# Two-batch gated cross-attention block on one core: 68 turns of the identity taken out of TensorE's order

## What is computed

```python
x = x + tanh(g_xattn[0]) * L0_xattn(ctx, layernorm(x), ...)   # 77 + 512 keys, 8 heads of 64, queries = tokens
x = x + tanh(g_ffn[0])   * L0_ffn(layernorm(x), ...)          # quantised linear 128->512, conv of 3, silu, quantised 512->128
x = x + tanh(g_xattn[1]) * L1_xattn(layernorm(x), ctx, ctx)   # 77 keys, 16 heads of 8, rotary
x = x + tanh(g_ffn[1])   * L1_ffn(layernorm(x), ...)          # 8 experts of 64, top 2, and a shared one
```

## The kernel before, in words

| place | turns | ahead of | bank |
|---|---|---|---|
| 1 | 8 | the first `k` projection (L592, L594) | 2 |
| 2 | 18 | `f1` of batch 1, its four turns of XN; an `a1` with two more follows | 7 |
| 3 | 5 | an `a4` front (L681) | 6 |
| 4 | 11 | an `a4` back (turns of S) | 2 |
| 5 | 5 | an `a4` back | 4 |
| 6 | 4 | an `a4` front | 4 |
| 7 | 11 | an `a4` back | 3 |
| 8 | 6 | an `a4` back | 2 |

## Time and profile before

### The profile page before, as it was taken

How to read it: one execution, slowest core, us unless ns; L and a number is a source line. 1 busy time by engine, 2 the same in 40 slices (tenths; PEclk the granted TensorE clock), 3 DMA queues, 4 the chain that set the end, 5 groups by cost and what they waited for, 6 DMA issues and landing times.

```text
span 271.9 us, 5419 instructions
## 1 busy us (share of the span) xinstructions
PE 248.7 (91%) x1754; PEld 183.7 (68%) x1754; DVE 230.7 (85%) x561; ACT 184.0 (68%) x462; POOL 32.3 (12%) x57
## 2 busy tenths in 40 slices
PE   0999999999999999999999999968868899899996
PEld 0757687787688866677678878745545565657665
DVE  5699969886679976999989789899999999998781
ACT  2596668776577557868879862159799596773561
POOL 3100000000001010000000021320002302133230
PEclk9999999999999999999999999999999999999999
DMA  6198620030300003300300000000000000000001
GB/s 203 38 251 298 159 58 2 0 91 0 91 0 1 4 0 89 91 0 4 89 0 4 0 2 0 4 0 0 1 2 2 2 0 4 0 10 4 29 0 41
DMA packets 8848, 10.70 MB, mean 39 GB/s; under 512 B 1115, under 2 KB 5877, under 8 KB 8821
## 3 DMA queue, kind: packets, MB, share of 16 engines
q1 hardware_dynamic: 7792, 9.70, 13.4%
q10 hardware_dynamic: 1029, 0.65, 0.8%
HBM read 4.99 MB, written 0.52 MB: 20 GB/s over the span
## 4 chain that ended last, share of the span: by engine, by line
PE 62%; DVE 23%; issue 7%; ACT 6%; DMA 1%; DVEq 0%; ACTq 0%
PE slot L535 18%; PE slot L621 11%; PE slot L602 6%; PE slot L603 5%; PE slot L580 3%; PE slot L762 3%; PE slot L628 2%; PE slot L586 2%; DVE nm L1063 2%; ACT S L916 2%; DVE mx L1172 2%; ACT PR L842 2%; PE slot L756 2%; PE slot L592 1%; PE slot L713 1%
## 5 line engine op out<-in xcount | busy, mean ns | idle before, releaser
L842 ACT ACTIVATE PR<-slot,nm 128x589 f32<-128x589 f32 x64 | 47.5, 749 | 14.7 <-DVE nm L1063 12.5
L1063 DVE TENSOR_REDUCE nm<-slot 128x1 f32<-128x589 f32 x64 | 46.4, 763 | 3.7 <-PE slot L603 3.2
L535 PE MATMUL slot<-K,PR 128*128 128x128 f32 (+1 forms) x320 | 44.4, 278 | 1.6 <-ACT PR L842 1.5
L535 PEld LDWEIGHTS slot<-K,PR 128*128 128x128 f32 (+1 forms) x320 | 35.5, 142 | 12.3 <-ACT PR L842 9.6
L602 PE MATMUL slot<-KH,Q 128*128 128x296 f32 (+1 forms) x128 | 40.7, 336 | 0.8 <-DVE PT L779 0.4
L621 PE MATMUL slot<-PT,V 128*64 128x256 f32 (+1 forms) x320 | 38.1, 384 | 0.0
L603 PE MATMUL slot<-KL,Q 128*128 128x296 f32 (+1 forms) x128 | 36.2, 299 | 0.0
L621 PEld LDWEIGHTS slot<-PT,V 128*64 128x64 f32 (+1 forms) x320 | 21.6, 137 | 11.9 <-issue 2.7
L602 PEld LDWEIGHTS slot<-KH,Q 128*128 128x128 f32 x128 | 24.1, 189 | 5.5 <-issue 2.1
L777 ACT ACTIVATE PT<-slot 128x640 f32<-128x640 f32 x34 | 23.5, 704 | 6.5 <-PE slot L535 5.8
L779 DVE COPY PT<-slot 128x640 f32<-128x640 f32 x30 | 24.4, 820 | 2.7 <-PE slot L535 2.3
(11 more groups left out here) (170 smaller groups left out, 500.8 us busy)
## 6 DMA issues: line engine op xcount, KB each, us to landing
KH<-KH SPq DMA_DIRECT2D x16, 147.5 KB, 2.5
KL<-KL SPq DMA_DIRECT2D x16, 147.5 KB, 2.5
CTT<-in_ctxT SPq DMA_DIRECT2D x1, 640.0 KB, 7.8
K<-in_const SPq DMA_DIRECT2D x1, 589.0 KB, 8.8
WGU<-in_wgu SPq DMA_DIRECT2D x1, 580.0 KB, 8.6
out<-X SPq DMA_DIRECT2D x8, 64.0 KB, 1.5
L1W<-in_l1w SPq DMA_DIRECT2D x1, 384.0 KB, 3.6
WD<-in_wdT SPq DMA_DIRECT2D x1, 320.0 KB, 11.3
```

Of the source, the lines that this page charges most:

```text
L535: return pe.transpose(dst, src, ident[0:p, 0:p])
L842: act.activation(PR[:, s, :], W[:, K0:K0 + KEYS0], ACT.Exp, bias=nm0[:, s:s + 1], accum_out=sum0[:, b, p * 2 + f, t, e:e + 1]).then_inc(pr ...
L1063: dve.tensor_reduce(nm0[:, s:s + 1], W[:, K0:K0 + KEYS0], AX.X, ALU.max, negate=True).then_inc(max_ready, 1)
```

## The change

The eight additions are cut from the words of `PLAN`; its later lines are wrapped anew, which makes the diff long, and no word changes its place. Two lines of it as they stood and stand:

```diff
-x0:F0 x0:A1 k:F2+8@2 x0:D2 q:F4 k:A1 k:F0 q:A1 k:D1 v:F6 x0:P2 k:A1 q:D1 v:F2 v:Ca k:D1 q:F5 v:Ca u:F6 x0:D3
+x0:F0 x0:A1 k:F2 x0:D2 q:F4 k:A1 k:F0 q:A1 k:D1 v:F6 x0:P2 k:A1 q:D1 v:F2 v:Ca k:D1 q:F5 v:Ca u:F6 x0:D3
...
-a3:P1 f4:B f4:B o:D1 a4:F2 f4:D2 a4:F0 n:P2 f4:D2 a4:F4 n:D3 f4:P2 f4:D3 f1:F6+18@7 a4:D1 a1:F7 f1:A1 a4:D1
+a3:P1 f4:B f4:B o:D1 a4:F2 f4:D2 a4:F0 n:P2 f4:D2 a4:F4 n:D3 f4:P2 f4:D3 f1:F6 a4:D1 a1:F7 f1:A1 a4:D1 a1:A1
```

More of the change, by code:

```diff
@@ L127 @@
 u:B u:Ca a3:F2 n:P2 u:Cd n:D3 w:F4 a3:D1 a3:F0 w:A1 w:D1 a3:P1 f4:F5 a3:D1 f4:F6 f4:A1 o:F7 f4:A1 o:F4 o:D1
-a3:P1 f4:B f4:B o:D1 a4:F2 f4:D2 a4:F0 n:P2 f4:D2 a4:F4 n:D3 f4:P2 f4:D3 f1:F6+18@7 a4:D1 a1:F7 f1:A1 a4:D1
-a1:A1 a4:A1 a2:F7 a1:P1 f1:D1 a2:D1 f2:F6 a4:A1 a4:B a4:D1 f2:A1 f2:F7 a4:D3 a4:Ca a4:B f2:A1 f2:D1 f2:F2
-f2:F3 a4:Ca f2:A1 a4:F0 f2:D1 f2:A1 f2:A2 f2:D1 a4:F6+5@6 f2:A2 a4:A1 f2:D1 f2:D2 a4:B+11@2 f2:D2 f2:A2
-a4:D1 f2:A2 a4:Ca a4:F2 f2:D2 a4:A1 f2:D2 a4:B+5@4 a4:D1 f3:F4 a4:Ca a4:D1 f3:F5 a4:A1 a4:F0 f3:D1 f3:D1
@@ new lines @@
+a4:A1 a2:F7 a1:P1 f1:D1 a2:D1 f2:F6 a4:A1 a4:B a4:D1 f2:A1 f2:F7 a4:D3 a4:Ca a4:B f2:A1 f2:D1 f2:F2 f2:F3
+a4:Ca f2:A1 a4:F0 f2:D1 f2:A1 f2:A2 f2:D1 a4:F6 f2:A2 a4:A1 f2:D1 f2:D2 a4:B f2:D2 f2:A2 a4:D1 f2:A2 a4:Ca
+a4:F2 f2:D2 a4:A1 f2:D2 a4:B a4:D1 f3:F4 a4:Ca a4:D1 f3:F5 a4:A1 a4:F0 f3:D1 f3:D1 f3:A1 a4:B a4:A1 f3:Cd
+f3:F4 a4:D3 f3:A1 a4:B a4:D3 a4:Ca f4:F5 f3:Ca a6:D0 f3:F6 f3:D1 a6:P1 f4:A1 f4:F7 f4:A1 f4:B f3:D1 f3:A1
+f4:B a4:Ca a6:F4 f4:D2 f3:A1 f4:D2 f3:Ca f3:Ca a4:D1 f4:F6 f4:P2 a6:A1 a4:F2 f4:A1 a6:D1 f4:F5 f4:D3 a4:A1
@@ new lines @@
+f4:B a6:B a4:D1 a1:F7 a6:D2 a1:A1 a4:B f4:A1 a1:P1 a4:A1 a2:F7 f4:D2 a6:P2 a4:Ca f4:B a2:D1 a4:B a4:Ca a6:D3
+a4:F6 f4:D2 m1:F4 a4:F0 a4:D1 m1:A1 f4:P2 m3:F2 a4:D1 a4:A1 a4:F4 m3:D1 a4:A1 f4:D3 a4:B a4:D3 m3:A1 a4:B
+a4:Ca a4:D3 a1:F3 a4:Ca m2:F6 a4:D1 a1:A1 m3:D2 a1:P1 a4:F0 a4:A1 m2:B a2:F3 a4:D1 m2:A1 a4:B m2:A2 m2:P1
+a2:D1 a4:A1 a4:Ca a4:B a6:D0 a4:F4 a4:D3 a6:P1 a4:Ca a6:F2 m2:D1 a6:D0 a4:D1 a4:F0 m2:D2 a6:A1 a6:P1 a4:A1
+a6:D1 a4:F6 a4:D1 a6:B a6:F3 a4:D1 a4:A1 a6:D2 a4:A1 a4:B a4:B a4:Cd a6:P2 a4:Cd a4:F4 a6:A1 a6:D3 a4:B
@@ new lines @@
+a6:D1 m1:F2 a4:D3 a4:Ca m4:F0 a4:D1 a6:B m1:A1 m4:A1 m3:F2 m2:F6 a6:D2 a4:A1 m4:B m2:A1 m2:P1 a4:D3 a4:B
+m4:D2 m2:B a6:P2 a6:D0 a4:Ca m3:D1 a6:P1 m2:F0 m2:A2 a6:D3 m3:A1 m2:F4 m2:A1 m2:D1 m3:D2 m1:F3 m2:A1 m2:B
+m1:A1 m2:B m2:A2 m2:D2 a6:F3 m2:P1 m2:A2 m2:P1 m2:D1 m4:F6 a6:A1 m2:D2 m3:F2 a6:D1 m4:A1 m4:F0 m2:D1 a6:B
+m3:D1 m4:A1 m4:B a6:D2 m3:A1 m4:B m4:D2 a6:P2 m2:D2 m2:F6 m4:D2 a6:D3 m4:F0 m3:D2 m2:A1 m2:B m4:A1 m1:F3
+m2:A2 m4:B m1:A1 m2:P1 m3:F4 m4:D2 m2:F2 m2:D1 m3:D1 m2:F0 m2:A1 m2:D2 m2:P1 m2:B m3:A1 m2:A1 m3:D2 m2:F6
@@ L147 @@
+m2:A2 m2:B m2:A1 m2:D1 m2:P1 m4:F4 m2:A2 m2:B m2:D2 m4:A1 m2:P1 m2:D1 m4:F2 m2:A2 m2:D2 m4:B m4:A1 m2:D1
+m2:D2 m4:F0 m4:D2 m4:B m4:A1 m4:F6 m4:D2 m4:B m4:A1 m4:B m4:D2 m4:D2
 """
```

## The result

The changed kernel took 276.86 us (median of 20 runs, 275.90 to 278.28), the kernel before 275.71 us (20 runs, 273.50 to 278.29). The ratio is 1.0054, 95% interval 1.0028 to 1.0080: slower, by about 1.5 us, and far inside 2%. It leaves out the three runs of the kernel before at 278.1 to 278.3 us, more than 1.5% above its fastest; over all runs the means are 276.8 and 275.9 us, 0.9 us apart. The forecast of 276.6 us in 273.2 to 282.5 holds. What stands behind it holds in part only, and the experiments show that the kernel before is not as steady as its one profile makes it look.

The account below looks back on a forecast made before the run. The prediction took VectorE and ScalarE, not TensorE, to set the pace around most of the turns. Its terms, -0.3 + 1.2 + 0.8 = +1.7 us, on the median 274.93 gave 276.6 us, range 273.2 to 282.5.

Parts of the forecast that it names:

- The seven later places: Sixty turns between 175.93 and 225.16 us; the next instruction waits for data, so removing them gains 0 as work.
- place 2: 18 turns from 175.93 to 177.95 us; gain 0 as work, but removal leaves a 3.2 us hole until 179.41.
- place 6: Four turns, the next instruction at 213.49 us after 0.93 us idle; gain 0.
- place 4: Eleven turns at 189.94 us, the next instruction at 191.61 waiting for ScalarE; gain 0, but removal leaves a 2.3 us hole.
- The clock falls in the new holes and soon mends: Likeliest case: a fall or two between about 179 and 191 us, each soon mended; 276.6 us, chance 0.48.
- the clock holds: Rival: TensorE's clock stays whole through the new holes; 274.5 us, chance 0.30.
- stays low to 208 us: Rival: the clock falls and stays low through the sparse part, 179 to 208 us; costs 7, 281.6 us, chance 0.20.
- if low clock reaches beyond 208 us: Sign that was to show the rival of a long low stretch, forecast at 281.6 us, chance 0.20.
- place 1: Eight turns before the first K projection, 7.62 to 9.32 us; removal gains 0.3, up to 0.6, or loses 1.4 net.
- The price of a fall: Low clock from 179.4 us costs 1.2 (bounds 0 to 3.3), from about 191 us 0.8 (bounds 0 to 1.8).
- L673's room: L673 at 180.96 us takes 0.9 us more at low clock; VectorE takes it up only at 182.90, cost next to 0.
- I put the change on the median: Whole kernel: adds +1.7 us to the runs' median of 274.93, not the profiled 273.79, giving 276.6 us.

Follow-up runs that it names:

- a kernel with 80 turns: The kernel before with 12 turns more in its longest hole, ahead of 198.97 us, against the kernel before: ratio 0.9970 (0.9926 to 1.0013).
- the full cover: The kernel before with turns added in every hole that has a free bank, against the kernel before: ratios 0.9967 and 0.9992; median 274.44 us in one set.

## Why the prediction was right or wrong

- **The seven later places bring nothing back as work: right.** Every instruction behind them still waits for the same data: 180.40 for VectorE's L1304, 189.94 for YC, 193.16 and 200.92 for ScalarE's S, 215.24 for Q. TensorE's idle time ahead of them grew by about what the turns had taken (1.08 to 2.87 us at place 2, 0.93 to 1.36 at place 6; at place 4 from 0.61 and 0.25 around the turns to 2.43).
- **The clock falls in the new holes and soon mends: right.** It was forecast for most executions and came in all 26 (by their mean clocks). The rival "the clock holds" is out by that, and the rival "stays low to 208 us", forecast at 281.6, by three stretches that each ended within 6.9 us in both profiled executions. The prediction's own sign for that rival, "if low clock reaches beyond 208 us", misleads here: it was low at 217.2 to 223.9, in a new fall behind 17 us at the whole clock.
- **"I take the gain of 0.3" at place 1: wrong in sign.** As work at an equal rise the eight turns were worth what the step said, 0.24 us for 0.3. But it took the rise to come at the same time, and in the profiled pair it came 2.4 us later, half of which is 1.2: a loss of 0.96, inside the bound of 1.4 that the step itself named. The experiments put the loss at about 0.5 us; why the rise came later stays open.
- **"Place 6, ... Gain 0" for places 6 to 8: incomplete.** As work, yes. As cover I looked only at places 2 to 4; the third fall stands at 217 us and is the dearest of the three, 0.8 us. TensorE has ten turns of S and two wide matmuls to do there almost without a hole (217.20 to 223.90, busy 6.35 of 6.70 us): it starts on them at 219.93, 1.76 us later than before, as far behind as ahead of the fall, and on the L680 behind them at 224.21, 3.43 later (before: 220.78); 0.9 of that is made up by 230.93.
- **The price of a fall: right in sum, wrong in its parts.** First fall 1.2 forecast, 0.56 measured; second 0.8, measured 0.2; third 0, measured 0.8. Together 2.0 forecast and 1.6 measured. The first was overpriced: the clock was low for 2.4 us of the f2 group (184.00 to 186.4), half of which is the 1.2, but the group grew by 0.74 us only (3.59 to 4.33), and 0.2 of that was made up by the turns of S behind place 4. Why it grew by less than half is not shown. The one slip ahead of it, L673's room, is small: RC L1158 waited 0.31 us for it, where I had "next to 0".
- **"I put the change on the median": this step carries the agreement, and part of it is luck.** Sum -0.3 + 2.0 = +1.7 us, measured in the profiled pair +2.6 and between medians +1.2 (276.86 less 275.71) to +2.6 (277.01 less 274.44). The forecast lies 0.3 us from the 276.86 measured because two errors went against each other: the sum was 0.9 us too low (the start 1.3 too low, the falls 0.4 too high), and it was put on 274.93, which lay 0.9 us above before's runs at a clock of 1.000 (274.0). What I did not see is that the median of before was itself made of executions with falls. "No row here shows a fall" was true of the one profile; the three run times, 273.53, 274.93 and 277.11, were the hint.
- **The rule of the Trainium skill.** The Trainium skill, "TensorE: Matmul & The Clock Gate", section "What's actually happening", says that the low clock is the default and that activity lifts it. These records agree: each low stretch (0.50 in the windows) began in or behind a stretch of TensorE's work with holes, and it ended 3.4 or 6.8 us later, with TensorE at work at 1.2 GHz. Its section "A second HAM failure mode: psum-queue depth-cycling" tells of a kernel in which frequent short pauses do it too; these records agree that no long pause is needed: the kernel without place 1 fell behind a hole of 1.65 us.

## What to carry to other kernels

A filler on TensorE is not judged by its busy time but by two questions: what the instruction behind it waits for, and whether the clock is held in all executions. One profile at a clock of 1.000 does not answer the second; the clock of every timed run does. And a filler that is as long as its hole turns into a delay as soon as the clock is low anyway (1.9 us for eleven turns here). In single executions half a cover can so be worth less than none: before's eight runs at 0.973 took 278.1 us, the changed kernel's at 0.963 276.4. Over all runs it was worth more than none here, and the full cover more than either.

## What the runs showed of the hardware that I had not expected

- A single kernel on one core, unchanged, has runs with mean clocks from 0.973 to 1.000 and times from 273.5 to 278.4 us, nearly in step with each other.
- Low stretches inside the work lasted 3.4 us (from 200.7, 217.6, 190.7 and 182.2, each in a kernel with most of its turns) or 6.8 us (in all three places of the changed kernel, but also from 216.3 in a kernel with 80 turns).
- The rise at the start came anywhere from 9.4 to 12.95 us, 3 to 6.5 us behind the first matmul, in kernels whose first matmul started within 0.2 us of 6.5.
